# A two-layer graph kernel on Trainium2: packing of the adjacency dealt by a table, up to three steps ahead of the products

## What is computed

```python
def layer0(X, adj, W, b):
    deg = clip(sum(adj, axis=1) + 1, 1)
    z = concat([X, (adj @ X + X) / deg], axis=1) @ W + b
    out = relu(z)
    return out / max(norm(out, axis=1), 1e-12)

def layer1(x, adj, W):                      # two hops
    for k in range(2):
        x = tanh(concat([adj @ x, x], axis=1) @ W[k])
    return x

x = layernorm(x + layer0(x, adj, W0, b))
x = layernorm(x + layer1(x, adj, W1))
```

## Time and profile before

| | us |
|---|---|
| median of 3 runs | 1273.65 (1273.53 to 1277.28) |
| the profiled execution, its own time | 1273.58 |
| its span, first to last instruction | 1271.7 |
| TensorE matmuls busy | 1195.5 (94%) |
| VectorE busy | 988.7 (78%) |
| ScalarE busy | 899.5 (71%) |
| GpSimd busy | 96.8 (8%) |
| 272.73 MB on the DMA queue that brings adj | 58.3% of the span, 16 engines |

### The profile page before, as it was taken

One profiled execution on the slowest core, in us unless ns is written; L12 is line 12 of the kernel. 1 busy time (PEld: TensorE's weight loads), 2 busy tenths in 40 slices (PEclk: granted clock), 3 DMA queues, 4 the chain that ended last, 5 costly groups with the idle time before them and its releaser, 6 DMA issues.

```text
span 1271.7 us, 25078 instructions
## 1 busy us (share of the span) xinstructions
PE 1195.5 (94%) x9510; PEld 819.7 (64%) x9510; DVE 988.7 (78%) x2641; ACT 899.5 (71%) x1310; POOL 96.8 (8%) x81
## 2 busy tenths in 40 slices
PE   3889989989999999999999999899999999999996
PEld 2445645645655655655655556778888888887775
DVE  7888898798898797798698687876655454778895
ACT  5778878778778678678668565675555555888783
POOL 3000020020020020010020011100000000010211
PEclk9899999999999999999999999899999999999998
DMA  9999999999999999899899880000000000000000
GB/s 322 381 385 370 372 377 364 366 381 356 364 374 375 343 350 379 319 355 361 309 359 346 322 323 4 1 1 1 1 1 1 1 1 1 1 9 9 18 17 19
DMA packets 88042, 274.64 MB, mean 216 GB/s; under 512 B 22384, under 2 KB 22384, under 8 KB 87920
## 3 DMA queue, kind: packets, MB, share of 16 engines
q1 hardware_dynamic: 86880, 272.73, 58.3%
q10 hardware_dynamic: 1040, 0.26, 0.1%
HBM read 270.88 MB, written 2.10 MB: 215 GB/s over the span
## 4 chain that ended last, share of the span: by engine, by line
PE 68%; DVE 15%; DMA 7%; POOL 4%; ACT 3%; issue 3%; DVEq 0%; POOLq 0%; ACTq 0%
PE acc L657 27%; PE acc L826 25%; DMA raw<-in_adj 7%; PE ps_pack L648 6%; DVE marks L905 6%; PE ps_epi L686 3%; ACT raw L467 3%; DVE planes L923 2%; PE ps_pack L788 2%; PE ps_pack L786 2%; POOL root L589 2%; DVE packed L910 1%; POOL root L582 1%; PE ps_epi L766 1%; PE ps_epi L801 1%
## 5 line engine op out<-in xcount | busy, mean ns | idle before, releaser
L467 ACT ACTIVATE raw<-raw 128x1024 f32<-128x1024 uint32 x512 | 535.8, 1048 | 193.2 <-DVE marks L905 192.0
L657 PE MATMUL acc<-planes,feats 128*128 128x512 fp8e4 x2512 | 569.1, 382 | 7.8 <-issue 7.8
L657 PEld LDWEIGHTS acc<-planes,feats 128*128 128x128 bf16 x2512 | 238.7, 98 | 279.6 <-issue 16.6
L905 DVE TENSOR_SCALAR marks<-raw 128x2048 uint8<-128x2048 f32 x256 | 314.4, 1241 | 26.2 <-DMA raw<-in_adj 25.8
L503 ACT ACTIVATE wide<-twos 128x2048 fp32r<-128x2048 fp8e4 x114 | 215.8, 1917 | 111.1 <-PE acc L826 100.8
L1129 DVE TENSOR_SCALAR wide<-twos 128x2048 fp32r<-128x2048 uint8 x114 | 139.4, 1223 | 74.8 <-PE acc L826 74.1
L648 PE MATMUL ps_pack<-pow,marks 128*128 128x64 bf16 x4096 | 141.8, 194 | 44.8 <-DVE marks L905 44.7
L648 PEld LDWEIGHTS ps_pack<-pow,marks 128*128 128x128 fp8e4 x4096 | 135.8, 98 | 67.7 <-issue 58.8
L923 DVE TENSOR_SCALAR planes<-packed 128x128 uint32<-128x128 uint32 x1024 | 150.9, 220 | 23.3 <-DVE packed L910 22.9
L826 PE MATMUL acc<-wide,x_high 128*128 128x512 f32 x512 | 126.7, 394 | 2.5 <-DVE wide L1129 2.2
L910 DVE TENSOR_SCALAR_CACHE_REDUCE packed<-ps_pack 128x512 uint8<-128x512 f32 x128 | 88.0, 687 | 36.8 <-PE ps_pack L648 36.6
(11 more groups left out here) (151 smaller groups left out, 960.5 us busy)
## 6 DMA issues: line engine op xcount, KB each, us to landing
raw<-in_adj SPq DMA_DIRECT2D x256, 1024.0 KB, 6.2
zpart<-in_x SPq DMA_DIRECT2D x7, 256.0 KB, 7.7
out<-result SPq DMA_DIRECT2D x7, 256.0 KB, 2.6
zpart<-in_x ACTq DMA_DIRECT2D x1, 256.0 KB, 9.2
out<-result SPq DMA_DIRECT2D x2, 128.0 KB, 2.0
w_own<-in_L_gnn_W SPq DMA_DIRECT2D x8, 16.0 KB, 6.5
w_a<-in_L_gnn_W SPq DMA_DIRECT2D x4, 16.0 KB, 6.6
w_y<-in_L_gnn_W SPq DMA_DIRECT2D x2, 16.0 KB, 6.7
```

What stands on the lines that cost most here:

```text
L467: ins = act.activation(words, words.bitcast(U32), ACT.Sign, accum_out=nonzero[:, tile:tile + 1, I])
L657: mm = pe.matmul(acc[g][:, h, :], feats[g][:, I * TB + a, :], planes[:, h, a, :], start=(start or g in opens) and a == 0, stop=a == TB - 1 ...
L905: dve.tensor_scalar(out_ap.bitcast(U8), raw[:, u, :], 1.0, 64.0, ALU.is_equal, ALU.mult).then_inc(marked, 1)
```

## The change

A table `PACKS`, made by `packing_order` when the program is built, says which packs TensorE and VectorE do in each step n: none, one or two, and at most as far as step n + 3. The planner replays a stream of data with constants of its own. ScalarE's copies of the sums are put behind the count that the table makes match. Here is the diff in full:

```diff
--- before.py
+++ after.py
@@ -154,6 +154,35 @@
 TURN_STEP = 12
 LN_EPS = 1e-5
 L2_EPS = 1e-12
+
+
+LOOKAHEAD = 3
+
+
+def packing_order():
+
+    packs, taken, pe, landed, packed_at = [], 0, 0.0, [0.0] * ALL, [0.0] * ALL
+    for n in range(ALL):
+        J, s = divmod(n, STEPS)
+        here = []
+        while taken + 1 < ALL and taken + 1 <= n + LOOKAHEAD and len(here) < 2:
+            p = taken + 1
+            landed[p] = max(landed[p - 1] + STREAM, packed_at[p - 2] + FREED if p > 1 else 0.0)
+            if p > n + 1 and landed[p] + MARKED > pe:
+                break
+            pe = max(pe, landed[p] + MARKED) + PACK
+            packed_at[p] = pe
+            here.append(p)
+            taken = p
+        packs.append(here)
+        heavy = ORDERS[J][s // 2] < J
+        pe += (HEAVY if heavy else LIGHT) + (WEIGH if J > 0 and s < TB else 0.0)
+    return packs
+
+
+STREAM, FREED, MARKED, PACK, LIGHT, HEAVY, WEIGH = 5.5, 3.0, 3.0, 1.1, 3.6, 5.3, 1.5
+PACKS = packing_order()
+TAKEN = [max(sum(PACKS[:n + 1], [0])) for n in range(ALL)]
 
 
 def gnn_kernel(nc, x, adj, w0, b0, w1, out):
@@ -483,12 +512,17 @@
                 act.wait_ge(epi_filled, USES_1 * J + 1)
                 act.activation(featT[:, :], ps_epi[:, :], ACT.Copy).then_inc(epi_drained, 1)
 
-            for J in range(NB):
-                for s in range(STEPS):
-                    count_step(J, s)
-                    if J > 0 and s < 2:
-                        save_acc(J - 1, s)
-                    if s == STEPS - 1:
+            def counts_before(n):
+
+                return min(TAKEN[n] + 1, ALL - 1)
+
+            for p in range(ALL):
+                count_step(p // STEPS, p % STEPS)
+                for J in range(NB):
+                    for h in range(2):
+                        if J < NB - 1 and counts_before((J + 1) * STEPS - 2 + h) == p:
+                            save_acc(J, h)
+                    if counts_before(J * STEPS + STEPS - 2) == p:
                         save_own(J)
             def low_bits(u):
 
@@ -703,8 +737,8 @@
                 for s in range(STEPS):
                     k, h = divmod(s, 2)
                     I = order[k]
-                    if J * STEPS + s < ALL - 1:
-                        pack(J, s + 1)
+                    for p in PACKS[J * STEPS + s]:
+                        pack(p // STEPS, p % STEPS)
                     pe.wait_ge(planes_ready, J * STEPS + (s + 1))
                     if k == 0 and J > 0:
                         pe.wait_ge(acc_saved, J * 2 + (h - 1))
@@ -905,8 +939,16 @@
                 dve.tensor_scalar(out_ap.bitcast(U8), raw[:, u, :], 1.0, 64.0, ALU.is_equal,
                                   ALU.mult).then_inc(marked, 1)
 
-            def save_pack(J, s, I):
-                dve.wait_ge(pack_done, J * STEPS + (s + 1))
+            def mark_next(p, pair):
+
+                if p + 1 < ALL:
+                    mark((p + 1) // STEPS, (p + 1) % STEPS, pair)
+
+            def save_pack(p):
+
+                J, s = divmod(p, STEPS)
+                I = ORDERS[J][s // 2]
+                dve.wait_ge(pack_done, p + 1)
                 dve.tensor_scalar(bytes_of(J, I, s % 2), ps_pack[:, :], 1.0, None, ALU.mult, ALU.add,
                                   accum_out=packsum[:, bass.ds((J * NB + I) * 2 + s % 2, 1)]).then_inc(pack_saved, 1)
 
@@ -1034,21 +1076,25 @@
                     dve.tensor_tensor(low, tiles(rest), mid, ALU.subtract).then_inc(x1_ready, 1)
 
             def block_one(J):
-                order = ORDERS[J]
                 for s in range(STEPS):
                     n = J * STEPS + s
-                    if n + 2 < ALL:
-                        mark(J, s + 2, 0)
+                    packs = PACKS[n]
+                    if packs:
+                        mark_next(packs[0], 0)
                     if J > 0 and 1 <= s <= TB:
                         drain(J - 1, s - 1, 1, USES_1 * (J - 1) + 1 + s)
+                    if packs:
+                        save_pack(packs[0])
                     if n + 1 < ALL:
-                        over = s + 1 == STEPS
-                        nxt = ORDERS[J + 1][0] if over else order[(s + 1) // 2]
-                        save_pack(J + 1, 0, nxt) if over else save_pack(J, s + 1, nxt)
                         dve.wait_ge(pack_saved, n + 2)
-                        expand(J + 1 if over else J, nxt, (s + 1) % 2, n if n > 0 else None)
-                    if n + 2 < ALL:
-                        mark(J, s + 2, 1)
+                        nxt = (n + 1) // STEPS
+                        expand(nxt, ORDERS[nxt][(s + 1) % STEPS // 2], (s + 1) % 2, n if n > 0 else None)
+                    if packs:
+                        mark_next(packs[0], 1)
+                    for p in packs[1:]:
+                        mark_next(p, 0)
+                        save_pack(p)
+                        mark_next(p, 1)
                     if J == 0 and s % 2 and s < STEPS - 1:
                         split_x((s + 1) // 2)
                     if J > 0:
@@ -1066,7 +1112,7 @@
             for pair in range(2):
                 mark(0, 0, pair)
             split_x(0)
-            save_pack(0, 0, 7)
+            save_pack(0)
             dve.wait_ge(pack_saved, 1)
             expand(0, 7, 0, None)
             for pair in range(2):
```

## The result

| | before | after |
|---|---|---|
| median, us | 1273.59 (4 runs) | 1298.82 (1297.40 to 1299.89, 4 runs) |
| ratio | | 1.0193 (95% interval 1.0174 to 1.0212) |
| the profiled execution, its time and span | 1273.58, 1271.7 | 1297.40, 1295.6 |

The account below looks back on a forecast made before the run. TensorE bounds from block 4 on; in blocks 1 to 3 stream and VectorE are near-bounds. Terms of 21.0, less 1.9 and 2.5, plus 6.7 for the clock, gave +23.3 us: 1297.0 us, range 1279 to 1306.

Parts of the forecast that it names:

- block 1, steps 23 to 25: Block 1, bound by VectorE and stream: marks of step 26 have data late, so work ends at 173.4 against 167.9, +5.5 us.
- steps 40, 41: Step 41 is block 2's counterpart of step 25; its missing pack was said to bring 0.1 us.
- late packs, shorter VectorE steps: Steps 125 to 127 have no packs, -1.9 us; expansions no longer wait for their save in VectorE-bound steps, -2.5 us.
- The coupling: One-pack steps need VectorE's marks from the step before at any lead, so blocks 4 to 6 keep their rhythm.
- The chain of 4.4 us: In two-pack steps the second pack waits for save, expansion and mark, starting 4.4 us behind the first; TensorE idles 3.4.
- The clock: Gaps of 3.4 us drop TensorE's clock behind each two-pack step, 1.7 us each; step 23's is hidden, so +6.7 us.
- Step 46: No pack needed, so the product may start when expansion 46 is done, about 285.0 against 287.24: gain 2.25 us.
- The wait for GpSimd: Steps 25 and 41: without marks to fill the time, VectorE idles 3 us ahead of `finish_one` 3, awaiting GpSimd's power.
- The sign for block 4: Sign of being right: blocks 3 and 4 start some 17 to 26 us later than 298.6 and 390.7.
- Without falls: Rival: the same forecast without falls of the clock, 1290 us; chance 0.20.
- The store: Rival: heavy steps let the stream run ahead and light ones live from it, 1259, likelier 1266 us; chance 0.11.
- Worse: Rival: late transfers hold back expansions in block 3's ten light steps, 13 us more, 1310 us; chance 0.06.

Follow-up runs that it names:

- e1: The changed kernel with LOOKAHEAD = 1, so one pack in every step: 1276.35 us beside 1274.89 of the kernel before, ratio 1.001.
- e6: The changed kernel with a table that has two packs only in steps 36 and 53: 1281.85 us, ratio 1.0054 to the kernel before.
- e5: The changed kernel with VectorE's mark for the second pack ahead of the expansion instead of behind it: 1286.27 us, ratio 1.0092.
- e3: The changed kernel with 14 matmuls of a zero block in the gap between the two packs of a step: 1288.89 us, ratio 1.0103.
- e8: The changed kernel with e6's table, packs after the first of step 36 behind the product, VectorE expanding for the next product first: 1310.05 us, ratio 1.0279.
- e10: The kernel of e8 with the row's operations ahead of VectorE's save and TensorE's packs behind the weighing: 1303.67 us, ratio 1.0222.
- e11: The kernel of e10 with VectorE's order turned to drain and row operations first, then expansion, first mark, save, second mark: 1283.80 us, ratio 1.0065.
- e7: The kernel before with VectorE's operation 3 right behind operation 2, so VectorE idles during GpSimd's power: 1294.06 us in one run.
- e4: The kernel before, lead 1, with VectorE's second mark ahead of its expansion: 1269.58 us, ratio 0.9948; again 1268.12 us, 0.9953.

## Why the prediction was right

The forecast was 1297.0 us, the result 1298.8. Step by step against the timelines (a price is the distance between the starts of the same steps, after less before; the blocks as a whole from the windows):

| place | predicted | measured |
|---|---|---|
| block 1, steps 23 to 25 | +5.5 | +2.1 (19.81 for 17.72), the whole block +3.1 |
| step 36 | +4.65 and 1.7 clock | +7.4 (14.39 for 7.01) |
| step 39 | +4.4 and 1.7 | +5.6 (10.86 for 5.28) |
| steps 40, 41 | -0.1 | -2.2 (7.84 for 10.01) |
| steps 45 to 47 | +2.15 and 1.7 | +8.5 (26.97 for 18.50) |
| step 53 | +4.4 and 1.7 | +6.8 (13.83 for 7.00) |
| late packs, shorter VectorE steps | -1.9 - 2.5 | -1.9 (block 7), -2.5 (blocks 4 to 6), -2.3 (block 3) |

The steps of block 2 that aren't listed cancel (+0.9 in step 35, -0.9 in steps 42 to 44).

- **The coupling** was right: one-pack steps keep their rhythm at any lead. e1 and e6 show that the price is that of the double steps, and blocks 4 to 7 lost nothing.
- **The chain of 4.4 us** was right: the second pack starts 4.2 to 4.5 us behind the first in steps 39, 47 and 53 (gaps of 3.1 to 3.4 us) and 5.1 us in steps 23 and 36, and e5 took the expansion's 1.1 us out of them.
- **The clock** was right in kind and too small. A fall here costs both the second pack (0.75 us) and the product (0.6 to 2.0 us): 10.6 us at steps 36, 39, 46, 47 and 53, against 6.7. I had taken the 1.7 us of block 0, and had not seen that step 46 could have a fall of its own. The Trainium skill (TensorE: Matmul & The Clock Gate, "The HAM clock gate") says that activity releases the throttle; e3 agrees, since busy work of no use kept the full clock.
- **Step 46** was wrong. "The product may start when expansion 46 is done": it also needs the rows of block 1, whose last operation VectorE does in step 45 (2.39 us of waiting, ended by line 1076; the changed kernel's timelines):

```profile
301.33 0.69 DVE L1076 TENSOR_TENSOR feats<-agg,feats 128x512 bf16<-128x512 f32 x1
302.12 6.91 PE L691 MATMUL acc<-planes,feats 128*128 128x512 fp8e4 x24 [2.39 <-DVE feats L1076]
```

  This wait had always been hidden behind the pack; taking the pack away uncovered it. With the fall behind it the place cost 4.6 us more than said.
- **The wait for GpSimd** (steps 25 and 41) was there, and 1.15 us long instead of 3. The sizes of the earlier trace rows are those of a GpSimd that runs beside a mark. With no mark beside it, only the expansion and then nothing, the power took 1.67 us (the changed kernel's step 25):

```profile
174.25 1.17 DVE L965 TENSOR_SCALAR planes<-packed 128x128 uint32<-128x128 uint32 x8
174.87 1.67 POOL L616 TENSOR_TENSOR root<-stat,minus_half 128x8 f32<-128x8 f32 x1
176.57 0.69 DVE L1032 SCALAR_TENSOR_TENSOR z<-z,root 128x512 f32<-128x512 f32 x1 [1.15 <-POOL root L616]
```

  VectorE's step 25, from its first operation to the first mark of step 26, takes 3.66 us (174.25 to 177.91), for 5.72 in the kernel before (167.84 to 173.56), and the two times are the same in block 2. That gave back 2.1 us in block 1, most of the 2.4 us by which the block came out cheaper, and 2 us in block 2, where the forecast had 0.1.
- **The sign for block 4** contradicted the sum. The sum has 27.7 us (21.0 and 6.7) by its start, the prediction named 17 to 26; it starts 28.1 us later (418.78 for 390.71). Block 3, at 23.5 us later, fits both.
- **Too large and too small terms** of some 5 to 8 us each cancelled. The total is closer than the terms deserve.
- **Rivals.** "Without falls" (1290) is what e3 made of it, 1288.9. The store (1259 to 1266) fell with the result, and again with e8, e10 and e11. "Worse" (late data in block 3) didn't come: block 3 rose by 4.5 us, less than its double step costs, and VectorE's waits for data in it are 4.3 us for 4.0 before.

## What to carry to other kernels

A lead of stored work is worth something only if the queue that builds it can run past the queue that uses it. Here both are written out in one order with two buffers between them, so building the lead costs a full turn of the chain with TensorE idle, and holding it brought nothing. Before moving work ahead, write down for one step what each engine waits for, and look for the instruction that stands in front of the critical one without need: one mark moved ahead of one expansion gave 0.5%, the table cost 1.9%. And price an idle gap of TensorE at its length and the clock behind it.

## What the runs showed of the hardware

- GpSimd's two small operations took 1.10 to 1.15 and 2.95 to 3.00 us beside VectorE's marks in blocks 1 to 4 and 6 of the kernel before, and 0.24 and 1.67 us with VectorE waiting (e7). Less than half. It is the marks that are in the way, and hardly the save or the expansion. In block 5 the second operation had a save and half an expansion beside it, but no mark, and took 1.71 us (rows below); in the changed kernel's step 25 an expansion alone left them at 0.36 and 1.67 us. And each long one of the kernel before ends 0.03 to 0.05 us behind the end of a mark, though it started well ahead of that mark: 172.19 in the earlier trace rows, where the mark ran from 170.93 to 172.15. The Trainium skill (GPSIMD Engine Reference, "Key points") says that GpSimd shares its SBUF interfaces with VectorE and contends with some kinds of its instructions; the rows agree, with the marks as such a kind.

```profile
541.25 1.71 POOL L582 TENSOR_TENSOR root<-stat,minus_half 128x8 f32<-128x8 f32 x1
541.54 0.69 DVE L910 TENSOR_SCALAR_CACHE_REDUCE packed<-ps_pack 128x512 uint8<-128x512 f32 x1 [0.47 <-PE ps_pack L648]
...
542.42 1.18 DVE L923 TENSOR_SCALAR planes<-packed 128x128 uint32<-128x128 uint32 x8 [0.18 <-DVE packed L910]
```

- Equal idle times of TensorE were followed by either clock: 2.4 us in front of product 46 by the low one in the changed kernel and by the full one in e3; 2.1 us in front of product 16 J + 14 of e10 by the full one in block 2 and by the low one in blocks 3 and 4. No run here shows what tells them apart.
- An expansion that stands right behind the save that it reads starts after 0.18 us of idle time; with a mark between the two the wait is gone (0.2 us in all in e4, 20.3 us in the kernel before).
